# Four-layer attention chain on one core: shorter first lead of the maxima, moved first transposes, and POOL loading head 1 in layers 1 and 2

## What is computed

```python
xn = group_norm(x)                                   # 32 groups
q = (x @ wq.T + bq)  # k and v alike, 8 heads of 32
scores = jnp.einsum('bhqd,bhkd->bhqk', q * scale, k)
attn = jax.nn.softmax(scores, axis=-1)
o = jnp.einsum('bhqk,bhkd->bhqd', attn, v)
out = o @ wo.T + bo + residual
```

## Time and profile before

| what | value |
|---|---|
| median of 3 runs | 469.26 us (469.04 to 471.65) |
| the profiled execution, its own time | 470.91 us |
| its span | 469.2 us |
| granted TensorE clock over the span | 0.983 |
| PE busy | 435.7 us |
| DVE busy | 368.4 us |
| ACT busy | 258.5 us |
| POOL busy | 215.0 us |

### The profile page before, as it was taken

The page is one execution under the profiler, slowest core; times in us unless marked ns, Lnnn a source line. Parts: engine busy times, 40 slices in busy tenths (PEclk is TensorE's granted clock), DMA queues, the critical chain, the costliest instruction groups (busy, mean ns, idle before and its releaser), DMA issues.

```text
span 469.2 us, 7016 instructions
## 1 busy us (share of the span) xinstructions
PE 435.7 (93%) x2210; PEld 241.2 (51%) x2210; DVE 368.4 (79%) x748; ACT 258.5 (55%) x515; POOL 215.0 (46%) x195
## 2 busy tenths in 40 slices
PE   8888999999896899999899999989999999998996
PEld 6544555554255475555445333657555455532463
DVE  7699998985777599997788486579998787848663
ACT  3238777775613337876677561224786676763032
POOL 8300031428010007899989911002799889971000
PEclk9989999999898999999999989999999999999998
DMA  5331545003300265589943530045378954550002
GB/s 158 52 69 25 159 67 134 23 5 68 70 0 0 58 146 113 125 181 193 212 105 61 112 68 3 1 108 128 79 165 173 198 110 81 110 96 25 0 1 89
DMA packets 20476, 41.87 MB, mean 89 GB/s; under 512 B 7278, under 2 KB 8566, under 8 KB 20184
## 3 DMA queue, kind: packets, MB, share of 16 engines
q1 hardware_dynamic: 15144, 25.41, 21.6%
q0 software_dynamic: 5152, 16.00, 18.4%
q10 hardware_dynamic: 144, 0.02, 0.0%
HBM read 8.30 MB, written 1.12 MB: 20 GB/s over the span
## 4 chain that ended last, share of the span: by engine, by line
PE 64%; DVE 14%; ACT 5%; POOL 4%; DMA 4%; SPq 4%; issue 3%; ACTq 0%; DVEq 0%; POOLq 0%
PE banks L1046 15%; PE banks L1035 14%; PE banks L1006 13%; DVE max L755 7%; PE banks L978 6%; DMA k_stack<-kL 4%; ACT E L610 3%; POOL SUMS L546 3%; DVE SUMS L784 3%; PE banks L1173 3%; PE banks L952 2%; PE banks L1061 2%; SPq L360 2%; SPq L353 2%; PE banks L1207 2%
## 5 line engine op out<-in xcount | busy, mean ns | idle before, releaser
L755 DVE TENSOR_REDUCE max<-banks 128x1 f32<-128x512 f32 x384 | 239.4, 683 | 32.9 <-PE banks L1006 32.0
L610 ACT ACTIVATE E<-banks 128x512 f32<-128x512 f32 x384 | 200.6, 616 | 44.3 <-PE banks L1035 42.0
L546 POOL TENSOR_TENSOR SUMS<-E 128x512 f32<-128x512 f32 x120 | 159.0, 1501 | 106.6 <-ACT E L610 106.5
L1006 PE MATMUL banks<-k_stack,q_stack 126*128 126x512 f32 x384 | 163.3, 439 | 8.5 <-DMA k_stack<-kL 6.2
L1035 PE MATMUL banks<-q_stack,k_stack 128*128 128x512 f32 x384 | 154.6, 413 | 5.7 <-ACT E L610 5.6
L1006 PEld LDWEIGHTS banks<-k_stack,q_stack 126*128 126x128 f32 x384 | 72.7, 191 | 44.4 <-DVE max L755 11.9
L1035 PEld LDWEIGHTS banks<-q_stack,k_stack 128*128 128x128 f32 x384 | 72.5, 191 | 41.6 <-ACT E L610 20.2
L1046 PE MATMUL banks<-E,V 128*32 128x512 f32 x768 | 93.6, 609 | 0.0
L1046 PEld LDWEIGHTS banks<-E,V 128*32 128x32 f32 x768 | 21.0, 111 | 47.5 <-issue 25.8
L599 ACT ACTIVATE mHL<-banks 8x128 fp32r<-8x128 f32 x48 | 12.7, 264 | 49.3 <-PE banks L1025 49.3
L521 POOL TENSOR_TENSOR att<-pv_sb,rec_sb 128x512 f32<-128x512 f32 x9 | 13.8, 1529 | 46.4 <-DMA rec_sb<-rec_rows 46.4
(11 more groups left out here) (149 smaller groups left out, 316.7 us busy)
## 6 DMA issues: line engine op xcount, KB each, us to landing
SUMS<-SUMS POOLq DMA_DIRECT2D x30, 512.0 KB, 4.9
k_stack<-kH SPq DMA_DIRECT2D x28, 128.0 KB, 2.3
q_stack<-qH SPq DMA_DIRECT2D x40, 64.0 KB, 2.0
rec_sb<-rec_rows SPq DMA_DIRECT2D x9, 256.0 KB
q_stack<-qH SPq DMA_DIRECT2D x16, 128.0 KB, 2.8
k_stack<-kL SPq DMA_DIRECT2D x14, 128.0 KB, 4.1
k_stack<-kH SPq DMA_DIRECT2D x22, 64.0 KB, 2.3
q_stack<-qL SPq DMA_DIRECT2D x20, 64.0 KB, 2.0
```

What stands on the lines that cost most here:

```text
L546: pool.tensor_tensor(SUMS[:, slot, :], E[:, E_PLAN[s][0], :], E[:, E_PLAN[s + 1][0], :], ALU.add).then_inc(sum_ready, 1)
L610: act.activation(E[:, slot, :], B[:, ring_of_scores(l, s) % B_RING, :], ACT.Exp, scale=1.0 if l == 0 else float(HEAD_DIM[l]) ** -0.5).then ...
L755: dve.tensor_reduce(max8[:, m % 2, 2 * t + half:2 * t + half + 1], A[:, A_PLAN[l][i][0], :], AX.X, ALU.max).then_inc(a_used, 1)
L1006: pe.matmul(A[:, bank, :], q_stack[0:SHIFT_ROW, slot, q0:q0 + P], k_stack[0:SHIFT_ROW, slot, k0:k0 + HALF], start=True, stop=True).then_in ...
```

## The change

It has four parts. The maxima lead by 14 tiles at first and grow by one at steps 1, 3, 5, 7, 9 and 11, to 20. The turns of the first three units stand at steps -5, 4 and 10 (before: -6, 2 and 10). The 16 late chunks of layers 1 and 2 stand at a written-out list of steps. And in layers 1 and 2 POOL, not SP, issues head 1's first loads, under a semaphore of its own, for which PE and ACT then wait.

```diff
-LEAD = 16
+LEAD = 14
...
-LEAD_GROWTH = (1, 3, 5, 7)
+LEAD_GROWTH = (1, 3, 5, 7, 9, 11)
+FIRST_ROWS = (-5, 4, 10)
...
 def rows_step(j):
-    return TILES * j - (10 if j > 2 else 6)
+    return FIRST_ROWS[j] if j < len(FIRST_ROWS) else TILES * j - 10
...
-        LATE_PE = [{}] + 2 * [{-15 + 2 * i: (4 + i // 2, i % 2) for i in range(16)}]
+        LATE_STEPS = (-14, -13, -11, -10, -8, -6, -4, -2, 1, 3, 5, 7, 9, 11, 13, 15)
+        LATE_PE = [{}] + 2 * [{s: (4 + i // 2, i % 2) for i, s in enumerate(LATE_STEPS)}]
...
+        def wait_stack(eng, l, h):
+            if l and h == 1:
+                eng.wait_ge(pool_stack, 16 * 6 * l)
+            else:
+                eng.wait_ge(stack_dma[h], stack_count(l))
...
-                for h in (1, 2):
+                for h in (2,) if l else (1, 2):
                     load_q(sp, l, h, first, stack_dma[h])
                     load_k(sp, l, h, both, stack_dma[h])
...
+                else:
+                    pool.wait_ge(b_done, STEPS * l)
+                    pool.wait_ge(high_ready, QK0[l] + 1)
+                    load_q(pool, l, 1, first, pool_stack, HIGH_Q)
+                    pool.wait_ge(split_ready, QK0[l] + 1)
+                    load_q(pool, l, 1, first, pool_stack, LOW_Q)
+                    pool.wait_ge(high_ready, QK0[l] + 3)
+                    load_k(pool, l, 1, both, pool_stack, HIGH_K)
+                    pool.wait_ge(split_ready, QK0[l] + 3)
+                    load_k(pool, l, 1, both, pool_stack, LOW_K)
...
-                        act.wait_ge(stack_dma[h], stack_count(l))
+                        wait_stack(act, l, h)
...
-                    pe.wait_ge(stack_dma[h], stack_count(l))
+                    wait_stack(pe, l, h)
```

More of the change, by code:

```diff
@@ L193, in attention_chain @@
         stack_dma = [sem(f"stack_dma{h}") for h in range(NH)]
-        half_dma = sem("half_dma")
+        half_dma, pool_stack = sem("half_dma"), sem("pool_stack")
         second_dma = [sem(f"second_dma{h}") for h in range(HEADS_B)]
```

## The result

| comparison on one chip | before, median (runs) | changed, median (runs) | ratio, 95% interval |
|---|---|---|---|
| first | 469.15 us (20) | 473.01 us (20) | 1.0075, 1.0057 to 1.0092 |
| again, beside the experiments | 469.77 us (35) | 471.35 us (12) | 1.0037, 1.0013 to 1.0060 |

By the ratio, the changed kernel is slower by 3.5 us in the first comparison (469.15 x 0.0075) and by 1.7 us in the second; the medians themselves lie 3.86 and 1.58 us apart. The forecast was +1.85 us. The two intervals barely touch, so a good part of the question is what makes the size differ from execution to execution. The profiled execution of the changed kernel took 472.19 us (span 470.2, granted clock 0.976).

A forecast was written before the change was run, and what follows sets the result against it. It took PE's order to decide, with VectorE nearly balanced and its idle time before tile 39 counting. 0.35 + 0.75 + 0.75 = +1.85 us on the median 469.26 gave 471.1 us; own range 470 to 472.5, 8 in 10 467.0 to 473.5.

The forecast's parts named there:

- What decides: Step 22, PE's turn of unit 4's maxima: VectorE's idle time before tile 39 counts, fewer tiles ahead save nothing.
- Layers 1 and 2, the chunks: Layers 1 and 2: five chunks ahead of tile 7 idle VectorE about 0.4 us three times; tile 39 0.75 later each.
- Layer 0: Layer 0: tile 9, now behind the first turn, reaches VectorE later, +0.35 us; tile 15 behind the first score, 0.
- The half clock rival: Layer 0: waits at the first two units' scores keep PE's clock low until step 22, +6.2 us, 477; chance 0.02.
- POOL's loads: Start of layers 1 and 2: tile 8's wait goes; sharing DMA engines delays tile 0 by 0 to 1.5 us, taken 0.
- The late loads rival: Layers 1 and 2: head 1's loads issued by POOL land late and hold tile 8, +3.9 us more, 475.0; chance 0.06.
- the signs: What would show the forecast in the profile, among them POOL's k loads landing within 4 us in layers 1 and 2.
- own range: Whole kernel: range of the forecast case itself, 470 to 472.5 us.
- the wide one: Whole kernel: the range for 8 in 10, 467.0 to 473.5 us.
- No net change: Layers 1 and 2: VectorE's early idles only match the 0.66 us a layer that goes, 469.3 us; chance 0.22.
- Faster: Layers 1 and 2: PE bounds, so the first score's 0.9 to 1.0 us gain carries through twice, 467.2 us; chance 0.15.

The follow-up runs named there:

- chunks in pairs: Kernel before with the new lead and turns in layers 1 and 2, one chunk behind every second tile, SP's loads: 469.45 us, ratio 1.0006.
- alone in layer 0: Kernel before with the lead of 14, its growth and the new turns in layer 0 only: 469.34 us, ratio 0.9992.
- every cost taken out: New lead and turns in all layers, with chunks behind every second tile, SP's loads and unit 1's shift issued earlier: 470.19 us, ratio 1.0026.
- early shift: Changed kernel with layer 0's shift of unit 1 issued ahead of the second q halves of heads 0 and 1: 472.19 us, ratio 1.0046.
- second profile: Profile of the changed kernel, unaltered, when measured again beside its variants: 471.35 us, ratio 1.0037 to the kernel before.
- layer 0's old order: Changed kernel with the old lead and old turns in layer 0 alone: 471.80 us, ratio 1.0045.
- the spread chunks: Changed kernel with its first eight chunks at steps -13, -11, -9, -7, -5, -3, -2 and -1: 475.05 us, ratio 1.0096.
- POOL's loads alone: Kernel before, but POOL issues head 1's loads in layers 1 and 2: 470.37 us, ratio 1.0009.
- held apart: Changed kernel with POOL's k loads of layers 1 and 2 waiting until head 0's second k half has landed: 473.69 us, ratio 1.0085.
- the list: Kernel before with only the new list of chunk steps, keeping lead 16, old turns and SP's loads: 470.23 us, ratio 1.0032.

## Why the prediction was right, and where it fell short

**What decides.** Right. The turn of unit 4 is where the order's cost is read, it still waits for VectorE, and the delays there add up to that of the whole to within 1.1 us.

**Layers 1 and 2, the chunks.** Right in place, way and size: three idles of 0.4, first score +10.94, tile 7 at +7.19, +0.69 a layer for +0.75. Tile 16 came 0.82 later in layer 2, as replayed; from there to tile 39 it was 17.7 us for the 17.8 forecast. (The prediction's own figures, 0.82 + 17.8 - 17.83, make 0.79, not 0.75.) With chunks in pairs the cost is gone.

**Layer 0.** The term was mis-sized. Tile 9's 0.35 is there where the clock at the first turn is 0.50: 0.38 in the changed kernel's first profile, alone in layer 0 and with every cost taken out. Where the clock is 0.81 or 1.00 (early shift, second profile) it is 0.08 to 0.09. The prediction took the low clock for the first turn at 25.98 from the stretch from 28 to 30; from 25.9 to 26.9 it was 0.75 in that profile. The step that failed is the look at shifts: the prediction asked of the shift of unit 0 how long it would hold the first score, and did not ask it of unit 1's for the score of step 8, which comes as much sooner, while SP's queue brings that shift at its old time. In the changed kernel that score waits 1.44 and 1.51 us, behind it the clock is low, and the term becomes 0.94 (0.38 and 0.56) and 1.16 (0.08 and 1.08). Waits of 0.68 and 0.69 in other kernels cost nothing. The half clock rival had the mechanism; at 477 us it overrated it, since the clock is back at 1.00 soon after.

**POOL's loads.** The step that failed is "I take 0" for the shared DMA engines, inside its bounds of 0 to 1.5. The reason that it gave holds for tile 0, which is no later, but it did not look at the second half, for which tile 4 waits. Head 0's second low half takes 4.56 us to land instead of 2.0 to 3.1, and the turn of layer 1 comes 0.87 us later on top of the order's 0.69 (1.56 in all), 0.78 in the kernel with layer 0's old order, 0.15 with the early shift, nothing in the changed kernel's second profile, where it lands in 3.6. In layer 2 of these it lands in 3.5 to 3.6, in time for a tile 4 that is due 3.45 us after tile 0 (in the kernels with the spread chunks and with POOL's loads alone, where tile 4 comes sooner, it waited in both layers). The late loads rival named POOL's own loads and tile 8; it was SP's load and tile 4. POOL's last k load did take 4.5 us in layer 1, over the 4 of the signs, and tile 8 did not wait for it.
By the rule that the prediction cited (the Trainium skill, "DMA: Bandwidth & Descriptors", Issuing engines are not separate DMA queues) a second issuer saves issue time only; the runs agree: held apart, SP's transfer lands in 2.8 us at most, beside POOL's in 3.5 to 4.6.

**The sum.** With the small values the three terms make 0.38 + 0.69 + 0.69 = 1.8 us, with the large ones 1.16 + 1.56 + 0.73 = 3.5. The forecast of 1.85 is the lower end: the order's cost without the two waits that come and go. The first comparison, +3.5 us, lies at the upper end, the second, +1.7, at the lower. The first median, 473.01 us, is above the prediction's own range (470 to 472.5) and inside the wide one by 0.5. That the second comparison agrees with the forecast to within 0.3 us is partly luck: in its profile the late shift is there, and the turns add up to 2.58. Whether the waits were more frequent in the first comparison is not shown, since only profiled executions can be looked into, nor whether the chip plays a part: the experiments ran on two. Of the three causes, only the order's is clear of noise in time when it is taken alone (the list, 1.5 us, 0.6 to 2.5); the price of the two waits is read from the turns.

**The rivals.** No net change falls with the idles. Faster falls too: in layer 2 the first score did come 0.87 sooner (+10.95 for +11.82), and the turn 0.68 later. No kernel here is shown to beat that before; the nearest, layer 0 alone (0.9992) and paired chunks (1.0006), cannot be told from it. With paired chunks the first score came at +10.47, 1.35 sooner than before, and the turn no sooner.

## What to carry to other kernels

When an order is shortened, every reader behind it comes sooner, not the first alone: hold each against the time at which its transfer's queue gets round to it. Two streams that are balanced to within 0.1 us a pair do not bear two extra pieces in a row ahead of the consumer's first unit, even if the total is the same. A load that is given to an idle engine competes with the load that everything waits for; hold its landing against the next reader on both queues.

## What the runs showed of the hardware that was not expected

The time that SP takes to issue one and the same transfer varies: a q load of layer 0 took 1.28 us in the changed kernel's profile and 0.59 in others, and a pair of them 2.66 instead of 1.22 in the kernel with spread chunks. In twelve of the fourteen profiles one issue within 17.5 us of layer 0's tile 0 took 1.03 to 2.02 us instead of at most 0.77, and not always the same one. Nothing in the trace says why. The wait at step 8 follows from it: with the new order in layer 0 and the shift in its old place, it was 1.44 to 2.21 us in the four profiles in which the long issue came ahead of the shift, and 0.68 and 0.69 in the two in which it came behind it.

The granted clock's low stretches differ between executions of like programs. In layer 0 from 28 to 30 us it was 0.50 in the changed kernel's first profile and 1.00 in its second. From 30 to 32, where before had 1.00, the first had 0.64, although its scores came sooner:

```profile
28.00:30.00 2.00, 2.00 (x6) 1.34 (x5) 2.00 (x5) 0.41 (x1) 0.00 (x0) 0.50 0.16 35
30.00:32.00 2.00, 2.00 (x7) 1.55 (x7) 1.93 (x6) 1.11 (x3) 0.00 (x0) 0.64 0.48 84
```

The prediction's reading of the Trainium skill ("TensorE: Matmul & The Clock Gate", What's actually happening), that earlier scores would release the clock sooner, is not borne out there.
